# A graph layer on one core: VectorE's step reordered, gathers issued by sides between the adds, ten triples for six, the last pair's roles exchanged

## What is computed

```python
h = jnp.maximum(_layernorm(x, axis=-1), 0.0)
x_ij = jnp.concatenate([h[src], h[dst]], axis=1)
m_ij = jax.nn.relu(x_ij @ W.T + b)          # W: 512 x 1024
return x + jax.ops.segment_sum(m_ij, src, num_segments=50000)
```

## Time and profile before

| | us |
|---|---|
| median of 3 runs | 740.08 (738.81 to 742.79) |
| profiled execution | 739.76 |
| its span | 737.9 |
| PE, DVE busy | 703.2, 593.8 |
| ACT, POOL busy | 470.1, 365.5 |
| mean granted clock of TensorE | 0.986 |

### The profile page before, as it was taken

How to read it: one execution, slowest core, us unless ns; L and a number is a source line. 1 busy time by engine, 2 the same in 40 slices (tenths; PEclk the granted TensorE clock), 3 DMA queues, 4 the chain that set the end, 5 groups by cost and what they waited for, 6 DMA issues and landing times.

```text
span 737.9 us, 12931 instructions
## 1 busy us (share of the span) xinstructions
PE 703.2 (95%) x3448; PEld 584.3 (79%) x3448; DVE 593.8 (80%) x2001; ACT 470.1 (64%) x892; POOL 365.5 (50%) x305
## 2 busy tenths in 40 slices
PE   3599999999999999999999999999999999999992
PEld 2478888888888888888888888888888888888881
DVE  6488888888888888888888888888888789777861
ACT  5377576576666757757667666675765766766640
POOL 7433233232232322323137777767777777777644
PEclk9799999999999999999999999999999999999997
DMA  7999999999999999999968787777878787878765
GB/s 250 398 380 378 365 377 351 348 365 356 362 362 369 364 368 359 356 376 353 362 146 136 148 135 150 131 144 130 145 139 143 141 142 143 139 148 133 134 87 71
DMA packets 35713, 182.36 MB, mean 247 GB/s; under 512 B 7018, under 2 KB 7342, under 8 KB 33048
## 3 DMA queue, kind: packets, MB, share of 16 engines
q0 software_dynamic: 29792, 77.00, 50.2%
q1 hardware_dynamic: 5504, 104.87, 37.5%
q10 hardware_dynamic: 392, 0.20, 0.1%
HBM read 156.44 MB, written 128.09 MB: 386 GB/s over the span
## 4 chain that ended last, share of the span: by engine, by line
PE 83%; DMA 4%; POOL 4%; issue 3%; ACT 3%; another core or an unknown queue 1%; DVE 0%; ACTq 0%; POOLq 0%
PE z_ps L639 22%; PE z_ps L637 22%; PE z_ps L638 21%; PE ht_ps L621 10%; DMA out<-ring,add_i 4%; PE agg_ps L646 4%; PE agg_ps L647 4%; POOL out L229 3%; POOL xg L209 1%; ACT w_hi L473 1%; ACT ht_hi L480 0%; ACTq L465 0%; ACT xg L496 0%; ACT xg L487 0%
## 5 line engine op out<-in xcount | busy, mean ns | idle before, releaser
L209 POOL DMA_INDIRECT xg<-x,node_i x196 | 204.8, 1045 | 264.4 <-PE ht_ps L621 218.3
L637 PE MATMUL z_ps<-w_hi,ht_hi 128*128 128x512 f32 x784 | 316.3, 403 | 8.4 <-DVE ht_lo L299 8.4
L639 PE MATMUL z_ps<-w_hi,ht_lo 128*128 128x512 f32 x784 | 309.4, 395 | 0.0
L638 PE MATMUL z_ps<-w_lo,ht_hi 128*128 128x512 f32 x784 | 307.6, 392 | 0.0
L480 ACT CAST ht_hi<-ht_ps 128x512 fp32r<-128x512 f32 x194 | 104.4, 590 | 215.6 <-PE ht_ps L621 184.9
L229 POOL DMA_INDIRECT out<-ring,add_i x98 | 158.3, 1615 | 101.3 <-DMA out<-ring,add_i 60.7
L637 PEld LDWEIGHTS z_ps<-w_hi,ht_hi 128*128 128x128 f32 x784 | 148.5, 189 | 36.9 <-DVE ht_lo L299 8.6
L639 PEld LDWEIGHTS z_ps<-w_hi,ht_lo 128*128 128x128 f32 x784 | 148.1, 189 | 32.5
L638 PEld LDWEIGHTS z_ps<-w_lo,ht_hi 128*128 128x128 f32 x784 | 148.4, 189 | 30.0
L496 ACT ACTIVATE xg<-xg,rstd 128x512 f32<-128x512 f32 x194 | 130.1, 725 | 1.9 <-issue 1.5
L299 DVE TENSOR_TENSOR ht_lo<-ht_ps,ht_hi 128x512 fp32r<-128x512 f32 x194 | 124.8, 685 | 8.0 <-ACT ht_hi L480 7.7
(11 more groups left out here) (64 smaller groups left out, 360.1 us busy)
## 6 DMA issues: line engine op xcount, KB each, us to landing
out<-x SPq DMA_DIRECT2D x125, 800.0 KB
xg<-x,node_i POOLq DMA_INDIRECT x196, 3.5
ring<-w_chunks SPq DMA_DIRECT2D x4, 512.0 KB, 4.7
out<-ring,add_i POOLq DMA_INDIRECT x98
row_lanes<-src_rows ACTq DMA_DIRECT2D x49, 4.0 KB
bias_bc<-bias SPq DMA_DIRECT2D x1, 256.0 KB
node_i<-node_cols SPq DMA_DIRECT2D x1, 98.0 KB, 1.9
```

The lines of the kernel that those rows point to most:

```text
L209: nc.gpsimd.indirect_dma_start(out=xg[:, b, s, :], out_offset=None, in_=x, in_offset=bass.IndirectOffsetOnAxis(ap=node_i[:, column:column ...
L637: nc.tensor.matmul(z_ps[b][:, :], hi, w_hi[:, c, :], start=(c == 0), stop=False)
L638: nc.tensor.matmul(z_ps[b][:, :], hi, w_lo[:, c, :], start=False, stop=False)
L639: last = nc.tensor.matmul(z_ps[b][:, :], lo, w_hi[:, c, :], start=False, stop=(c == K - 1))
```

## The change

In words: `TRIPLES` is 10, so that the last thirty tiles ahead of the last pair are ten triples, and 33 pairs come before. VectorE's step adds the bias of s-1 first, then makes the statistics of s+2 and waits for them, compares the rows of s-1, and only then makes the moments of s+2; the rest of its step is as before. GpSimd's gathers are issued one side at a time: after each pair's adds 17/8 of a side on average (2 or 3), after each triple's adds 3; and a tile from the fourth on waits, in addition to its slot, for the transposes of tile (t-3)//2. The last pair exchanges roles: 96 takes the second place and 97 the first, so that 96's sum needs only itself and 97's sum takes both; the last group's two adds wait each for its own tile. VectorE's `same_source` gets a branch for tile 96 that spreads the row numbers in exchanged order, and ScalarE stores 96's sum ahead of its last step. The diff, cut to what is spoken of:

```diff
-    TRIPLES = 6
+    TRIPLES = 10
+    RAMP = 4
@@ place
-            if not isinstance(t, int) or t < FIRST3 or t >= TILES - 2:
+            if not isinstance(t, int) or t < FIRST3:
                 return b, t - b, 2
+            if t >= TILES - 2:
+                return 1 - b, t - b, 2
@@ gpsimd
-            def gather(t):
+            def gather_side(t, s):
                 b = t % XS
-                if t >= XS:
-                    pool.wait_ge(transposed, SIDES * (t - XS + 1))
-                if t == 0:
+                if s == 0 and t >= RAMP:
+                    pool.wait_ge(transposed, SIDES * (max(t - XS, (t - RAMP + 1) // 2) + 1))
+                if t == 0 and s == 0:
                     pool.wait_ge(nodes_loaded, 16)
-                for s in range(SIDES):
...
-                pool.wait_ge(add_ready, first + size)
+                if group < len(GROUPS) - 1:
+                    pool.wait_ge(add_ready, first + size)
                 for t in range(first, first + size):
+                    if group == len(GROUPS) - 1:
+                        pool.wait_ge(add_ready, t + 1)
...
             for t in range(FIRST_ADD):
-                gather(t)
-            added = 0
-            for t in range(FIRST_ADD, TILES):
-                while added < t - FIRST_ADD + 1 and sum(GROUPS[added]) <= t - 7:
-                    add(added)
-                    added += 1
-                gather(t)
-            for group in range(added, len(GROUPS)):
+                for s in range(SIDES):
+                    gather_side(t, s)
+            gathered = SIDES * FIRST_ADD
+            for group, (first, size) in enumerate(GROUPS):
                 add(group)
+                if size == 3:
+                    wanted = gathered + 3
+                else:
+                    wanted = SIDES * FIRST_ADD + 2 + min(group, 2) + group * 17 // 8
+                while gathered < min(wanted, SIDES * TILES):
+                    gather_side(gathered // SIDES, gathered % SIDES)
+                    gathered += 1
@@ vector, add_bias
                 dve.wait_ge(mm_done, t + 1)
-                if not isinstance(t, int):
-                    dve.wait_ge(stats_done, SIDES * (t + 4))
@@ vector, step
-                if has(2):
-                    statistics(s + 2, (m + 2) % XS)
                 if has(-1):
                     add_bias(s - 1, 1 - b)
                 if has(2):
-                    aggregate(s + 2, b)
+                    statistics(s + 2, (m + 2) % XS)
+                    dve.wait_ge(stats_done, SIDES * (s + 3))
                 if has(-1):
                     same_source(s - 1, (m - 1) % XS)
+                if has(2):
+                    aggregate(s + 2, b)
@@ tensor
-            def first_half_of_last_pair(t):
+            def first_of_last_pair(t):
...
+                sum_of(1, ((2, 1),))
+                nc.tensor.matmul(agg_ps[0][:, :], same[:, 1, :], m_hi[:, 1, :], start=True, stop=False)
+                nc.tensor.matmul(agg_ps[0][:, :], same[:, 1, :], m_lo[:, 1, :], start=False, stop=False)
+            def second_of_last_pair(t):
...
+                nc.tensor.matmul(agg_ps[0][:, :], same[:, 0, :], m_hi[:, 0, :], start=False, stop=False)
+                pe.wait_ge(mlo_ready, t + 1)
+                nc.tensor.matmul(agg_ps[0][:, :], same[:, 0, :], m_lo[:, 0, :], start=False, stop=True
```

More of the change, by code:

```diff
@@ L199, in _ @@
         def _(pool):
-            def gather(t):
+            def gather_side(t, s):
                 b = t % XS
-                if t >= XS:
-                    pool.wait_ge(transposed, SIDES * (t - XS + 1))
-                if t == 0:
+                if s == 0 and t >= RAMP:
+                    pool.wait_ge(transposed, SIDES * (max(t - XS, (t - RAMP + 1) // 2) + 1))
+                if t == 0 and s == 0:
                     pool.wait_ge(nodes_loaded, 16)
-                for s in range(SIDES):
[L208 to L213, removed]
+                column = s * TILES + t
+                nc.gpsimd.indirect_dma_start(
+                    out=xg[:, b, s, :], out_offset=None, in_=x,
+                    in_offset=bass.IndirectOffsetOnAxis(ap=node_i[:, column:column + 1], axis=0),
+                    bounds_check=last_node, oob_is_err=False
+                ).then_inc(first_arrived[s] if t == 0 else x_arrived[b], 16)
             def add(group):
@@ L318, in same_source @@
                     dve.wait_ge(row_spread, t + 1)
+                elif isinstance(t, int) and t == TILES - 2:
+                    dve.wait_ge(row_arrived[m // 2], 2 * (t - m) + 16)
+                    for half in range(2):
+                        nc.vector.stream_shuffle(src_row[:, half * P:(half + 1) * P],
+                                                 row_lanes[:, m // 2, (1 - half) * P:(2 - half) * P], [0] * LANES
+                                                 ).then_inc(row_spread, 1)
+                    dve.wait_ge(row_spread, t + 2)
                 elif b == 0:
@@ L458, in _ @@
             dve.wait_ge(agg_done, TILES)
-            nc.vector.tensor_copy(ring[:, (TILES - 1) % RING, :], agg_ps[1][:, :]).then_inc(last_filled, 1)
+            nc.vector.tensor_copy(ring[:, (TILES - 1) % RING, :], agg_ps[0][:, :]).then_inc(last_filled, 1)
         @block.scalar
@@ L605, in _ @@
                     step(s + d, (RING + 3 + d) % XS, again=True)
-            for s in range(RING + 3 + XS * rounds, TILES + 1):
+            for s in range(RING + 3 + XS * rounds, TILES):
                 step(s, s % XS, again=True)
             act.wait_ge(scattered, 16 * (TILES - RING))
-            store_sum(TILES - 2, 0, True)
+            store_sum(TILES - 2, 1, True)
+            step(TILES, TILES % XS, again=True)
         @block.tensor
@@ L677, in first_half_of_last_pair @@
                 pe.wait_ge(mlo_ready, t + 1)
[L678 to L690, removed]
+                sum_of(1, ((2, 1),))
+                nc.tensor.matmul(agg_ps[0][:, :], same[:, 1, :], m_hi[:, 1, :], start=True, stop=False)
+                nc.tensor.matmul(agg_ps[0][:, :], same[:, 1, :], m_lo[:, 1, :], start=False, stop=False)
+            def second_of_last_pair(t):
+                pe.wait_ge(same_ready, t + 1)
+                pe.wait_ge(mhi_ready, t + 1)
+                nc.tensor.matmul(agg_ps[0][:, :], same[:, 0, :], m_hi[:, 0, :], start=False, stop=False)
+                pe.wait_ge(mlo_ready, t + 1)
+                nc.tensor.matmul(agg_ps[0][:, :], same[:, 0, :], m_lo[:, 0, :], start=False, stop=True
                                  ).then_inc(agg_done, 1)
@@ L728, in _ @@
             products(TILES - 1, 1, (0,))
-            first_half_of_last_pair(TILES - 2)
+            first_of_last_pair(TILES - 2)
             products(TILES - 1, 1, (1,))
-            second_half_of_last_pair(TILES - 2)
+            second_of_last_pair(TILES - 1)
 def kernel(x, src, dst, L0_gnn_W, L0_gnn_b):
```

## The result

| | before | after |
|---|---|---|
| median of the timed runs | 740.19 us (735.44 to 744.15) | 743.69 us (742.43 to 758.65) |
| ratio, 95% interval | | 1.0055 (1.004 to 1.0069) |
| profiled execution, its span | 739.8, 737.9 | 743.8, 742.0 |

The kernel is slower by 3.5 us, 0.55%. The forecast had the sign, and its whole range (739 to 754) holds the time, but at 749.6 it had 2.7 times the loss. The time falls 0.3 us short of its narrower range (744 to 754), and 0.1 us short of the 743.8 above which it had put 0.67 of its chances.

A forecast was written before the change was run, and what follows sets the result against it. Before was taken to end by GpSimd's add chain, with TensorE 2.8 us ahead. TensorE's 2.7 + 8 + 3.3 = 14.0, less that slack, gave +11.2; less 1.4 at the start, 739.8 became 749.6 us (own range 744 to 754, whole 739 to 754).

The forecast's parts named there:

- four more triples: TensorE's matmuls: three tiles cost 0.68 us more in a triple than in pairs, times 4, 2.7 us in all.
- VectorE's order: VectorE's step ends later and TensorE's sums wait for its low part: 8 us in nine triples, 3.3 in 33 pairs.
- the start: TensorE's stall from 22.8 to 31.18 us: holding back gathers of tiles 5 to 8 might shorten it; 1.4 us gain taken.
- TensorE's slack before: Last triple in before: its first sum was stored 2.8 us ahead of the add, so TensorE could lose that much free.
- The bound: End of before: GpSimd's chain of adds, each waiting for the landing of the one before, arrives just behind TensorE.
- The forecast gain: GpSimd's add chain: ten triples for six save 5.7 us, third gathers cost 2 (0 to 8) of it.
- my row of 0.3 to 1.4 more: GpSimd's groups with a third gather: each loses about 0.3 us, 1.4 at most without the idle time before landing.
- The last pair: Exchanged roles of the last two tiles: nothing counted, up to 1 us lost if the last triple's landing no longer covered it.
- The signs that I had named: Profile after: sums waiting for the low part, reciprocals 1.1 us (pair) and 1.9 (third tile) later, triple steps over 21.88 us.
- the doubtful term: Pair's sum on TensorE, delayed by VectorE's path: 0.1 us each, 3.3 us in 33 pairs, bounds 0 and 8.
- the rival in which it goes: Stall at the start goes with the gathers: 751.0 - 8.4 - 1.6 = 741 us; chance 0.22.
- the one in which VectorE's order is free as well: No stall at the start and no cost of VectorE's order: add chain bounds at 736.1 us; chance 0.08.

The follow-up runs named there:

- E9: Kernel before with the last 50 of the 125 copies of x left out, so that TensorE alone bounds the end: 728.92 us.
- E11: Kernel after with VectorE's old order and the last 50 of the 125 copies of x left out: 731.52 us.
- E10: Kernel after with the last 50 of the 125 copies of x left out: 743.66 us.
- E2: Kernel after with VectorE's old order (statistics, bias, moments, comparison), all copies kept: 745.33 us, ratio 0.9966 to before on the same chip.
- E7: Kernel after with the low part of message s-1 moved ahead of the scales and low parts of the activations: 742.53 us, ratio 0.9956 to before.
- E1: Kernel after with the old throttle on the gathers, each waiting only for its slot: 745.59 us, ratio 0.9992 to before.
- E4: Kernel before with VectorE's new order alone, gathers and TensorE's program untouched: 746.22 us, ratio 1.0005 to before.
- E12: Kernel before with one always fulfilled wait on GpSimd ahead of the gathers of tiles 4 to 7: 744.64 us.
- E5: Kernel after, unchanged, repeated on another chip: 747.76 us, ratio 1.0012 to before.
- E8: Kernel after with VectorE's old order and 14 triples instead of 10, ScalarE's second loop written out: 739.76 us, ratio 0.992 to before.

## Why the prediction was right or wrong

Set up with TensorE's marks, from E9, E11 and E10 and the two first profiles:

| step | forecast, us | measured, us | from |
|---|---|---|---|
| four more triples | +2.7 | +2.8 | 709.34 - 706.54 |
| VectorE's order | +11.3 | +12.4 | 721.77 - 709.34 |
| the start | -1.4 | -9.1 | 706.54 - 715.62 |
| TensorE's slack before | -2.8 | -1.95 | below |
| end of the kernel | +9.8 | +4.2 | sum; spans: 742.0 - 737.9 = 4.1 |

**The bound** was read rightly: before ends by its adds, with TensorE's last sums only just ahead of them. The slack was 0.85 us too large. I let the add start as soon as the sum was stored; after shows that it starts 723.12 - (721.62 + 0.59) = 0.91 us behind the store (E9: 707.92 - 707.13 = 0.79). In before it could have started at 717.1, and did at 719.07.

**Triples, gathers, last pair.** The matmuls of the four triples came to their price. The chain of adds was never tested in after, where it doesn't bind; in E2 and E7 it does. From the first add to the last triple E2 takes 340.7 us and E7, with the same GpSimd program, 385.41 to 721.5 = 336.1, against 341.8 in before. The forecast gain was 5.7 - 2 = 3.7; measured are 1.1 and 5.7. Pairs with a third gather took 8.01 us in E2 and 7.87 in E7 (for 7.50), within my row of 0.3 to 1.4 more. Why the two differ by 4.6 isn't settled. The last pair cost nothing, as said: from the last triple's add to the end it is 742.0 - 723.12 = 18.9 us, and 737.9 - 719.07 = 18.8 before.

**VectorE's order** held in mechanism, place and size. Its parts: a pair loses 14.28 - 14.13 = 0.15 us for 0.1, times 33 = 5.0 for 3.3; a triple 22.6 - 21.84 = 0.75 us for 0.9, times nine = 6.8 for 8; the first steps some 0.6. The signs that I had named are there: reciprocals 3.73 us behind a pair's transposes (predicted 3.81) and 4.26 in a triple's third tile (4.56, because VectorE was free earlier than I had it), the sum's matmul behind its low part, triples longer than 21.88. The pair was the doubtful term. Its own path had given 556.15 - 556.03 = 0.12 us, taken as 0.1, and TensorE loads the sum's weights 0.12 us behind the low part's end (629.68 to 629.80), where I had 0.06. There the Trainium skill (VectorE: DVE Perf Modes, "The DRAIN you can't avoid") has a semaphore behind an instruction cost nothing. In after the statistics start at 617.31 and the shuffle that waits for them at 618.63: 1.32 us for two whose pitch is 0.61, so the awaited second one took 0.71. The page's measurement is of copies with a semaphore after each; for an instruction that the next one waits for, the trace has 0.1 us more than the rule, as the 0.72 of the earlier trace rows had said. A pair's loss of 0.15 us is of about that size; whether it would go with that wait wasn't tested.

**The start** is the step that failed. Of a stall of 8.4 us and its clock I took 1.4, with the start "much as it was", and gave 0.22 to the rival in which it goes (0.30 with the one in which VectorE's order is free as well). It went wholly, 9.1 us by the marks (8.8 at tile 6 between the two first profiles, 62.28 - 53.44). The rival forecast 741: with its 10 us replaced by 9.1, the order's 1.1 more and the slack's 0.85 less it gives 751.0 - 9.1 + 1.1 + 0.85 = 743.85, and the profiled time is 743.8. That the rival's number is this close doesn't confirm its reason, the gathers. They don't make the stall alone (they are issued at once in E1, E4, E9 and E12, without it), and what the engines wait for is no gather but TensorE's own signals, which come up to 8.5 us late. But the long stall is there in both profiles of before and in none with the throttle, and all profiles of the old gathers without it come from two chips on which no kernel had late signals. Whether the throttle, another part of the change, the chip or the single execution took it away is open, and so is what holds the signals back. That after had no such stall doesn't hang on one profile: its 18 runs lie between 742.43 and 744.97 us and E10's eight between 743.22 and 744.47, which leaves no room for 9 us in any. Of before the timed runs can't tell how often the stall came, since they end by the adds.

**How the two nearly cancelled.** By TensorE the change costs 15.2 us (12.4 + 2.8), and the vanished stall gives 9.1 of it back. Neither shows in the time of before, which goes by its adds: there the stall was covered all but 1.95 us. That is why the difference is 3.5 us where the adds start at 377, and nothing that shows where they start at 382 to 387: before moves with the copies' end by the whole 6 us, while after, whose adds stood waiting for TensorE (12.34 us at the last triple), moved by less, 4 us in E5.

## What to carry to other kernels

When an in-order engine's work is reordered, follow the operand that the busiest engine waits for to its place in the queue: it was the low part at the end of VectorE's step, not the moved statistics, that cost 0.15 us a pair and 0.75 a triple, and moving that one operation ahead brought pairs and triples back to 14.15 and 21.89 us. Where two chains end within 2 us of each other, make each one's end a number of its own (here by cutting the copies) before judging an edit, because the time shows only the later of the two. And a stall whose releaser the trace doesn't name should be carried at its full price as well as at nothing, not as a small mean, and its size be read at a mark just behind it (here tile 6), before anything else has moved TensorE. Whether an edit removed it can only be said beside the unchanged kernel, profiled on the same chip: here that comparison is missing, and without it E12 proves less than it seems to.

## What the runs showed of the hardware that I had not expected

- TensorE's signals can be late. Increments that normally come 0.3 to 0.4 us behind the matmul's start came 6.9 to 8.5 us behind it in both profiles of before, three within 0.12 us (29.73 to 29.85 and 29.24 to 29.36), and 1.5 to 4.6 us behind it in E5, E7 and E8. All four profiles on one chip have this, the eight on two others don't. GpSimd stood 2.8 and 2.3 us by it in before, ScalarE 7.8 and 7.3.
- The same copies end at different times: first add at 376.3 to 377.3 us in the first two profiles, at 381.7 to 386.7 on the three chips of the experiments, and at up to 5 us apart on one and the same of them (381.75 in E5, 386.72 in E8). With it the time of before, bound by its adds, moved from 740 to 747 us.
- An awaited statistics instruction takes 0.71 us where the pitch without a wait is 0.61, and a sum that starts with a late weight load has its second matmul 0.34 us behind that load (629.80 to 630.14) instead of the usual 0.23.
